# Moving softplus sums to TensorE and a share of the C products to GpSimd in a fused Mamba and SwiGLU kernel

## What is computed

```python
u = _silu(conv(xs));  delta, Bm, Cm = split(u @ x_proj_w.T, [64, 80])
delta = softplus(delta @ dt_proj_w.T + dt_proj_b)
deltaA = exp(einsum('bld,dn->bldn', delta, A))
deltaB_u = (delta * u)[..., None] * Bm[:, :, None, :]
state = dA * state + dBu                  # over the 512 tokens
y = einsum('bdn,bn->bd', state, c)
y = (y + u * D) * _silu(res);  x = layernorm(x + y @ out_proj_w.T + x)
x = layernorm(x + (silu(x @ wg.T) * (x @ wu.T)) @ wd.T)
```

## Time and profile before

| | |
|---|---|
| median of 3 runs | 580.98 us (580.44 to 583.85) |
| the profiled execution | 581.86 us, span 580.1 us |
| mean granted TensorE clock | 0.898 of full speed |
| busy, of 580.1 us | VectorE 521.0, TensorE 476.2, GpSimd 417.0, ScalarE 367.2 |
| one scan of a group, VectorE | 1.21 us, 256 times |
| one product of a quad, GpSimd | 4.54 us, 63 times |
| one decay, ScalarE | 0.69 us (three in a row 1.91) |
| table load, SiLU of 128x512, Copy of 128x512, ScalarE | 1.28, 0.68, 0.60 us |
| C spread and B spread, TensorE, one record | 0.50 us, 0.42 from start to start |
| x1 part of the job down, 8 records | 1.05 us |
| filler, TensorE | 348 records, 102.5 us |

### The profile page before, as it was taken

How to read it: one execution, slowest core, us unless ns; L and a number is a source line. 1 busy time by engine, 2 the same in 40 slices (tenths; PEclk the granted TensorE clock), 3 DMA queues, 4 the chain that set the end, 5 groups by cost and what they waited for, 6 DMA issues and landing times.

```text
span 580.1 us, 6345 instructions
## 1 busy us (share of the span) xinstructions
PE 476.2 (82%) x1887; PEld 239.6 (41%) x1887; DVE 521.0 (90%) x562; ACT 367.2 (63%) x581; POOL 417.0 (72%) x214
## 2 busy tenths in 40 slices
PE   8988774989979996989978996989888996587574
PEld 6332431535542553534442553444443452243243
DVE  5869789998999899998999899999999899999924
ACT  3577865489458866589458866589458855544220
POOL 8758597857695796968695796868695796876010
PEclk9889976989979898989979897989979997769879
DMA  8063333600642032600551042501451042500000
GB/s 222 3 146 62 83 72 74 145 1 5 141 108 56 1 82 67 160 1 15 131 120 46 0 97 62 149 0 24 121 131 31 0 101 70 138 1 0 1 18 18
DMA packets 27368, 39.22 MB, mean 68 GB/s; under 512 B 3816, under 2 KB 10056, under 8 KB 27344
## 3 DMA queue, kind: packets, MB, share of 16 engines
q1 hardware_dynamic: 25424, 38.51, 27.9%
q10 hardware_dynamic: 1920, 0.42, 0.4%
HBM read 3.27 MB, written 2.10 MB: 9 GB/s over the span
## 4 chain that ended last, share of the span: by engine, by line
PE 27%; issue 23%; DVE 21%; POOL 18%; ACT 6%; DMA 2%; SPq 1%; POOLq 0%; DVEq 0%; ACTq 0%
DVE state L1038 14%; POOL prod L864 10%; PE dense_ps L464 6%; PE dense_ps L482 5%; PE y_ps L456 4%; DVE weighted L1046 3%; POOL z_wm L868 2%; ACT decay_ps L620 2%; POOL z_wm L870 2%; PE c_ps L442 1%; PE dense_ps L484 1%; PE dense_ps L506 1%; POOL z_wm L881 1%; PE dense_ps L502 1%; SPq L358 1%
## 5 line engine op out<-in xcount | busy, mean ns | idle before, releaser
L864 POOL TENSOR_TENSOR prod<-du_rep,b_rep 128x2048 f32<-128x2048 f32 x63 | 285.6, 4540 | 52.0 <-ACT b_rep L657 32.8
L1038 DVE TENSOR_TENSOR_SCAN state<-decay_ps,prod 128x512 f32<-128x512 f32 x256 | 299.1, 1207 | 19.5 <-ACT decay_ps L620 13.4
L620 ACT ACTIVATE decay_ps<-delta_rep,a_neg 128x512 f32<-128x512 f32 x252 | 170.6, 688 | 107.3 <-DVE state L1038 107.1
L1046 DVE TENSOR_TENSOR weighted<-state,c_ps 128x2048 f32<-128x2048 f32 x64 | 146.4, 2288 | 4.2 <-PE c_ps L442 2.3
L464 PE MATMUL dense_ps<-x_all,ident 128*128 128x256 f32 x348 | 102.5, 430 | 18.9 <-ACT bc L653 9.4
L464 PEld LDWEIGHTS dense_ps<-x_all,ident 128*128 128x128 f32 x348 | 67.1, 207 | 65.9 <-issue 21.2
L456 PE MATMUL y_ps<-weighted,gather 128*32 128x512 f32 x512 | 77.7, 683 | 17.0 <-DVE weighted L1046 17.0
L482 PE MATMUL dense_ps<-h_t,tap_t 128*128 128x512 f32 x128 | 58.5, 599 | 0.9 <-ACT h_t L668 0.9
L442 PE MATMUL c_ps<-bc,pick 64*128 64x512 f32 x64 | 34.7, 542 | 19.7 <-DVE weighted L1046 19.7
L442 PEld LDWEIGHTS c_ps<-bc,pick 64*128 64x128 f32 x64 | 12.8, 200 | 69.6 <-issue 38.5
L889 POOL TENSOR_TENSOR ve<-mv,epsm 128x4 f32<-128x4 f32 x14 | 2.8, 202 | 53.1 <-DVE mv L1057 53.1
(11 more groups left out here) (148 smaller groups left out, 628.6 us busy)
## 6 DMA issues: line engine op xcount, KB each, us to landing
du_rep<-z_wm SPq DMA_DIRECT2D x64, 256.0 KB, 4.7
delta_rep<-z_ln SPq DMA_DIRECT2D x64, 256.0 KB, 4.5
out_dram<-y_out SPq DMA_DIRECT2D x8, 256.0 KB, 2.2
state<-L_attn_in_proj_w_in ACTq DMA_DIRECT2D x1, 256.0 KB, 3.9
x_all<-L_attn_x_in SPq DMA_DIRECT2D x1, 256.0 KB, 4.3
weighted<-L_ffn_w_gate_in SPq DMA_DIRECT2D x1, 192.0 KB, 9.8
weighted<-L_ffn_w_up_in SPq DMA_DIRECT2D x1, 192.0 KB, 3.5
weighted<-L_ffn_w_down_in SPq DMA_DIRECT2D x1, 192.0 KB, 4.5
```

The lines of the kernel that those rows point to most:

```text
L620: A(decay_ps[n % DECAYS][:, :], decay_ps[n % DECAYS][:, :] if spread_first else delta_rep[:, h, c, :], ACT.Exp, scale=a_neg[:, col:col + 1 ...
L864: TT(prod[quad % 2][:, :, :], du_rep[:, h, :, :], b, ALU.mult).then_inc(prod_ready, 1)
L1038: dve.tensor_tensor_scan(state[n // BLOCKS % 2][:, n % BLOCKS, :], decay_ps[n % DECAYS][:, :], prod[n // BLOCKS % 2][:, n % BLOCKS, :], 0. ...
L1046: TT(weighted[quad % 2][:, :, :], state[quad % 2][:, :, :], c_ps[:, :].unsqueeze(1).broadcast_to([P, BLOCKS, T]), ALU.mult).then_inc(weigh ...
```

## The change

The same computation with another division of labour:

- Delta is summed by TensorE: two new jobs d0 and d1 add the four parts in PSUM by four products with the identity, and ScalarE copies the result out. `zwm` now gives 1 - w instead of w - 1. GpSimd's `error` and `soften` stay for the head alone.
- C is multiplied onto the state in place; `weighted` is gone. So a quad's first scan waits until the quad two before has been summed, where the multiply waited for that so far.
- In quads 0, 1, 4 and 5 GpSimd multiplies the first of the four blocks (`weigh_first`), from an SBUF copy of C that ScalarE makes at quads 0 and 1 (`hold_c`); VectorE multiplies the other three.
- PLAN, BANK, ACT_AT, DVE_AT, POOL_AT and the head's fillers are new. The 23 fillers of a steady batch become 5.

```diff
-        weighted = pair("weighted", [P, BLOCKS, T])
+        c_rep = sb("c_rep", [P, CHUNKS, T])
-        cut = room(weighted[0][:, :, :])
+        cut = room(state[1][:, :, :])
-        PLAN = [["Fh", "h", "S", "C", "proj", "xs0"],
...
+        PLAN = [["h", "C", "S", "proj"],
+                ["xs0", "C", "S", "Fxs1"],
+                ["xs1", "res0", "C", "res1", "S"],
+                ["xd", "Fz0", "Fz0", "C", "z0", "Fz1", "S", "z1", "Fx1", "x1"],
+                ["S", "gate0", "C", "d0"],
+                ["C", "S", "gate1", "up0", "d1", "gate2"],
+                ["S", "b0", "C", "up1", "up2", "down", "b1", "b2", "b3"],
+                ["S", "C"]]
+        BANK = {"h": 2, "xs0": 1, "proj": 2, "xs1": 0, "res0": 2, "res1": 1, "xd": 0, "z0": 2, "z1": 0, "x1": 0,
+                "gate0": 2, "up0": 0, "gate1": 2, "up1": 1, "gate2": 2, "up2": 0, "b0": 0, "b1": 1, "down": 2,
+                "b2": 2, "b3": 1, "d0": 0, "d1": 1}
+        ACT_AT = {"hx": 0, "y": 8, "h": 0, "r1": 5, "silu": 10, "xd": 11, "x1n": 14, "z": (14, 15), "x1": 18,
+                  "ze": 18, "zw": 19, "zwm": 19, "ln": 20, "gate": (19, 22, 25), "b": (26, 29, 29, 30), "down": 27,
+                  "d": (21, 25), "c": 2}
+        DVE_AT = {"combine": (17, 2), "stats1": 9, "gate": (19, 23, 25), "up": (24, 26, 26), "stats2": 29}
+        POOL_AT = {1: ["C0"], 2: ["C1"], 3: ["norm1"], 4: ["low"], 5: ["C4", "scale0"], 6: ["C5"], 7: [],
+                   8: ["scale1", "norm2"]}
+        STIR_HEAD = {"h": 12, "xs0": 1, "du0": 3}
+        SHARED = [0, 1, 4, 5]
+        HELD = sorted({quad % CHUNKS for quad in SHARED})
+        def shares(quad):
+            return sum(q < quad for q in SHARED)
             def spread_c(it, quad):
                 it.wait(pe, weighted_ready, QUADS, 0, quad)
+                if quad > 0 and quad - 1 in HELD:
+                    it.wait(pe, c_held, len(HELD), 0, HELD.index(quad - 1) + 1)
             def sum_states(it, quad, batch=0):
...
+                if quad in SHARED:
+                    it.wait(pe, share_ready, len(SHARED), batch, shares(quad + 1))
...
+                elif kind == "d":
+                    it.wait(pe, z_step, 4, 1, 3)
+                    mm(ps[:, :], ident[:, :], z_e[:, n, :], start=True, stop=False)
+                    it.wait(pe, wm_ready, 1, 1, 1)
+                    mm(ps[:, :], ident[:, :], z_wm[:, n, :], start=False, stop=False)
+                    it.wait_taken(pe, f"z{n}")
+                    mm(ps[:, :], ident[:, :], z_pos[:, n, :], start=False, stop=False)
+                    it.wait(pe, ln_ready, 1, 1, 1)
+                    last = mm(ps[:, :], ident[:, :], z_ln[:, n, :], start=False, stop=True)
+            def take_delta(it, h):
+                name = f"d{h}"
+                it.wait_full(act, name)
+                it.take(A(delta[:, h, :], it.ps(name)[:, :], ACT.Copy), name)
+            def hold_c(it, q):
+                it.wait(act, c_ready, QUADS, 0, q + 1)
+                it.wait(act, share_ready, len(SHARED), -1, shares(q + CHUNKS + 1))
+                A(c_rep[:, q, :], c_ps[:, :], ACT.Copy).then_inc(c_held, 1)
-                        A(z_wm[:, :, :], z_w[:, :, :], ACT.Copy, bias=-1.0).then_inc(wm_ready, 1)
+                        A(z_wm[:, :, :], z_w[:, :, :], ACT.Copy, scale=-1.0, bias=1.0).then_inc(wm_ready, 1)
+            def weigh_first(it, quad):
+                it.wait(pool, scanned, GROUPS, 0, BLOCKS * quad + 1)
+                it.wait(pool, c_held, len(HELD), 0, HELD.index(quad % CHUNKS) + 1)
+                TT(state[quad % 2][:, 0, :], state[quad % 2][:, 0, :], c_rep[:, quad % CHUNKS, :], ALU.mult
+                   ).then_inc(share_ready, 1)
             def scan(it, n):
                 if n % BLOCKS == 0:
-                    it.wait(dve, weighted_ready, QUADS, 0, n // BLOCKS - 1)
+                    it.wait(dve, summed, QUADS, 0, n // BLOCKS - 1)
+                    if it.k0 == 0 and n == BLOCKS:
+                        dve.wait_ge(ffn_float, 3)
             def weigh(it, quad, batch=0):
-                it.wait(dve, summed, QUADS, batch, quad - 1)
                 it.wait(dve, c_ready, QUADS, batch, quad + 1)
-                TT(weighted[quad % 2][:, :, :], state[quad % 2][:, :, :],
-                   c_ps[:, :].unsqueeze(1).broadcast_to([P, BLOCKS, T]), ALU.mult).then_inc(weighted_ready, 1)
+                if quad in HELD:
+                    it.wait(dve, c_held, len(HELD), batch, HELD.index(quad) + 1)
+                mine = slice(1 if quad in SHARED else 0, BLOCKS)
+                TT(state[quad % 2][:, mine, :], state[quad % 2][:, mine, :],
+                   c_ps[:, :].unsqueeze(1).broadcast_to([P, BLOCKS - mine.start, T]), ALU.mult
+                   ).then_inc(weighted_ready, 1)
```

More of the change, by code:

```diff
@@ L220, in mamba_swiglu_postln @@
         weighted_ready = sem("weighted_ready")
+        c_held = sem("c_held")
+        share_ready = sem("share_ready")
         summed = sem("summed")
@@ L239, in mamba_swiglu_postln @@
         y_free = [sem(f"y_free{i}") for i in range(2)]
-        PLAN = [["Fh", "h", "S", "C", "proj", "xs0"],
[7 rows of a table removed]
-        BANK = {"h": 1, "xs0": 1, "proj": 2, "xs1": 0, "res0": 2, "res1": 1, "xd": 2, "z0": 0, "z1": 2, "x1": 0,
-                "gate0": 1, "up0": 2, "gate1": 0, "up1": 1, "gate2": 2, "up2": 0, "b0": 0, "b1": 1, "down": 2,
-                "b2": 0, "b3": 2}
-        ACT_AT = {"hx": 0, "y": 9, "h": 0, "r1": 5, "silu": 10, "xd": 13, "x1n": 14, "z": (15, 16), "x1": 18,
-                  "ze": 17, "zw": 18, "zwm": 19, "ln": 21, "gate": (19, 20, 21), "b": (24, 28, 29, 30), "down": 28}
@@ L255, in mamba_swiglu_postln @@
-        DVE_AT = {"combine": (21, 2), "stats1": 9, "gate": (19, 21, 22), "up": (20, 23, 25), "stats2": 29}
-        POOL_AT = {1: [], 2: [], 3: ["norm1"], 4: ["low"], 5: ["error0", "error1", "soften0"],
-                   6: ["soften1", "scale0"], 7: [], 8: ["scale1", "norm2"]}
-        STIR_HEAD = {"h": 11, "xs0": 2, "du0": 2}
+        PLAN = [["h", "C", "S", "proj"],
[6 more added lines that the diff above has]
+                ["S", "C"]]
@@ L320, in wait_free, with wait_delta @@
                     eng.wait_ge(taken[self.bank(name)], value)
+            def wait_delta(self, eng, h):
+                if self.k0 < 0:
+                    eng.wait_ge(delta_ready, h + 1)
+                else:
+                    self.wait_taken(eng, f"d{h}")
             def ps(self, name):
@@ L455, in sum_states @@
                 for c in range(BLOCKS):
-                    last = mm(y_ps[DB * c:DB * c + DB, :], gather[:, :], weighted[quad % 2][:, c, :],
+                    last = mm(y_ps[DB * c:DB * c + DB, :], gather[:, :], state[quad % 2][:, c, :],
                               start=False, stop=(q == CHUNKS - 1), tile_position=(0, DB * c))
@@ L683, in dense @@
                         if step == at["z"][h]:
-                            if h == 0:
+                            if h == 0 and it.k0 == 0:
                                 it.wait(act, delta_ready, HALVES, 0, HALVES)
@@ L706, in dense @@
                     A(z_ln[:, :, :], z_e[:, :, :], ACT.Ln, bias=1.0).then_inc(ln_ready, 1)
+                if it.ins:
+                    for h in range(HALVES):
+                        if step == at["d"][h]:
+                            take_delta(it, h)
+                if it.scan and step % BLOCKS == at["c"] and step // BLOCKS in HELD:
+                    hold_c(it, step // BLOCKS)
                 if it.k0 == 0:
@@ L877, in scale_u @@
             def scale_u(it, h):
-                it.wait(pool, delta_ready, HALVES, 1, h + 1)
+                it.wait_delta(pool, h)
                 if h == HALVES - 1:
@@ L929, in iteration @@
                             scale_shift(it, mv2, mv2_ready, ve2, nm2, ve2_ready, rs2, rs2_ready, nmr2, shift2_ready)
+                        if name[0] == "C" and it.scan and int(name[1]) in SHARED:
+                            weigh_first(it, int(name[1]))
                         if name == "low" and it.ins:
@@ L932, in iteration @@
                         for h in range(HALVES):
-                            if name == f"error{h}" and it.ins:
-                                error(it, h)
-                            if name == f"soften{h}" and it.ins:
-                                soften(it, h)
                             if name == f"scale{h}" and it.ins:
```

2 lines of the change are left out of this document (1 added, 1 removed), and 7 rows, old and new, of the table PLAN.

## The result

| | before | after |
|---|---|---|
| median, runs alternating on one chip | 581.44 us (578.69 to 584.54) | 586.64 us (584.77 to 587.45) |
| profiled span | 580.1 us | 584.9 us |
| mean granted TensorE clock | 0.898 | 0.843 |

What follows compares the result with a forecast made beforehand. It took VectorE as full, with TensorE, ScalarE and GpSimd queues arriving with under 0.2 us to spare. 1.0 - 6 x 0.2 - 1.6 + 1.2 = -0.6 from 581.86 gave 581.3, median 580 us; range 566 to 592, the forecast's own 575 to 587.

Steps and rivals of the forecast that it cites:

- 1, scan 4: Scan 4 still waits for GpSimd's product 1, T+7.45 (T: start of scan 0); quad 0's saving is lost.
- 2, scan 8: Four scans (4.59 us) and a narrower multiply (2.21 less 0.53) put scan 8 at T+13.7.
- 3, scan 12: Quad 2 as before, 7.93 us without its wait: scan 12 at T+21.65.
- 4, xd copy: ScalarE copies xd at T+21.7, before at T+23.54; scan 13 therefore waits 0.5 to 0.9 us.
- 5, logarithm ends: ScalarE takes 16.95 us from xd copy to logarithm, formerly 18.66; it ends at T+38.65, 3.5 us earlier.
- 6, stall of 1.7 before scan 22: Scan 22's decay, behind logarithm and table load, is ready at T+40.6; VectorE, there at T+38.9, stalls 1.7 us.
- 7, scan 24: GpSimd's product 6 follows delta copy 0 and scale0, ending T+46.95; scan 24 at T+47.05, before T+48.79.
- 8, up2 taken; down's end: TensorE's queue behind the logarithm takes 17.1 us: up2 done on VectorE at T+52.85, down ends T+55.9.
- 9, product 0; period: ScalarE's copies and decays reach T+59.9, then product 0 ends at T+64.5; period 64.6 us, 0.2 less.
- Rival 1: VectorE stays the bound, waits stay 3.1 us per batch: 566 us in full, 573 by half; chance 0.28.
- rival 2: TensorE falls to half clock after idling, delaying delta products or the queue behind: period 66.3, 591 us; chance 0.3.
- Rival 3: Narrow in-place multiplies don't pay, costing 0.5 us more a quad: 583 to 587 us; chance 0.07.

Runs made afterwards that it cites:

- e6: Changed kernel, but in batch 0, quad 0, VectorE multiplies all four blocks and GpSimd none: 585.53 us, ratio 1.0099 to the kernel before.
- e3: Changed kernel with six more filler jobs on TensorE between z1 and the x1 filler: 586.31 us, ratio 1.0096 to the kernel before.
- e9: Kernel before with only the in-place C multiply shared with GpSimd; softplus, TensorE order and fillers as before: 584.82 us, ratio 1.0088.
- e12: e9 without the ten TensorE fillers between gate product 2 and up product 2: 582.85 us, ratio 1.0036 to the kernel before.
- e2: Changed kernel with the share undone, VectorE multiplying all four blocks of every quad with C: 588.57 us, ratio 1.0137 to the kernel before.
- e5: Changed kernel with gates and ups going round three PSUM banks in the closing batch alone: 583.31 us, ratio 1.0059 to the kernel before.
- e7: Changed kernel without three of the four products of delta job 1 (less than the whole computation): 597.53 us, ratio 1.031 to the kernel before.

## Why the prediction was wrong

The sign was wrong: 1 us faster was forecast, 5 slower came. The steps that failed are terms of the sum that were mis-sized: batch 0 (+1.0, measured +2.29), the six periods (-1.2, measured +1.18), the last scanned batch (-1.6, measured -0.63) and the closing one (+1.2, measured +1.96). Behind them stands a reading that was wrong as well, of what bounds the kernel.

**The steps of the period.** Measured against T = 167.57, in the order of the prediction:

| step | predicted | measured |
|---|---|---|
| 1, scan 4 | T+7.45 | T+7.41 |
| 2, scan 8 | T+13.7 | T+13.68 |
| 3, scan 12 | T+21.65 | T+21.55 |
| 4, xd copy | T+21.7 | T+21.77 |
| 5, logarithm ends | T+38.65 | T+38.95 |
| 6, stall of 1.7 before scan 22 | yes | no: VectorE had lost 1.82 at the combine |
| 7, scan 24 | T+47.05 | T+47.44 |
| 8, up2 taken; down's end | T+52.85; T+55.9 | T+53.3; T+56.3 |
| 9, product 0; period | T+59.9; 64.6 | T+60.42; 64.99 |

The mechanism was right: GpSimd behind the copy of delta, TensorE's queue behind the logarithm. The products queued behind it took 17.3 us (206.57 to 223.83) where 17.1 were worked out. The sum is late by 0.3 us at the logarithm (step 5), 0.4 at scan 24 and 0.5 at product 0. Over the five periods from batch 2 on the mean is 64.88 us, 64.83 before: +0.05 where -0.2 was forecast, 1.3 us of the error. The first period, 65.68, is 0.9 longer than before and makes 1.1 more; it was taken to be like the others, and what lengthens it is open (e6 only shows that it grows when batch 0 ends sooner). The text had said that "0.5 us in one is 3 us", and took the middle. Step 6's stall was right in kind: e3 shows it, at 1.73 us, where the clock is repaired.

**The analysis of the bound failed.** "VectorE is full, but three queues arrive with less than 0.2 us to spare" takes the queues for guests. e9 shows them to be the bound: with 1.9 us less on VectorE the period is 64.80 as before. Rival 1, at 0.28, deserved next to nothing, and the chance of slower more. The 3.1 us of waits in the earlier trace rows were the mark: an engine that waits 3.1 us in each turn is not the longest path by itself, the path is one that runs through those waits. In the rows that I had, product 0 waited 4.99 us for a b_rep copy; I noted it as nearly late, and it is on one of the paths that close. TensorE ran at half clock from 319 to 322; I used that for rival 2 alone, and by e12's short batches it was worth, with the stretch behind the beat, 2.1 us of every period of e9. In steady batches, then, the change could only gain by its order and by the clock. Its order brought 3.3 us at the logarithm and gave them back in d0, d1 and the sums queued behind it, as steps 7 and 8 said.

**The ends** make 3.0 of the 5.4 us of error. Batch 0 was sized at +1.0 and measured +2.29. The block of quad 0 costs its 1.23 us as worked out, but the u x delta of half 1 comes 1.98 us later than in the earlier trace rows, at 52.47: scan 3 is 0.73 us later, and GpSimd's first addition waits for VectorE's work behind it. Its decay stands on ScalarE behind h_t, which waits 2.69 us for TensorE where it waited 1.56; why TensorE comes later there is open, but it goes with the share: in e9 scan 3 is 0.51 us later, in e2, without the share, 0.41 us earlier (40.04), and there nothing of the 2.29 is left. In the changed kernel nothing comes back; scan 16 starts 1.91 us later (70.28):

```profile
42.80 1.28 POOL L914 TENSOR_TENSOR z_wm<-z_e,z_wm 128x512 f32<-128x512 f32 x1 [1.62 <-DVE z_wm L1075]
...
45.38 1.27 POOL L932 TENSOR_TENSOR state<-state,c_rep 128x512 f32<-128x512 f32 x1
...
52.47 1.27 POOL L927 TENSOR_TENSOR z_wm<-z_ln,u 128x512 f32<-128x512 f32 x1
```

The last scanned batch gave -0.63 where -1.6 was due; e9 gives exactly 1.6 with TensorE's old order, so the missing 1.0 us is the new order's (waits of 0.38 us for a C spread and 0.36 for a tanh, which e9 does not have; the other 0.2 is not located). The closing batch was predicted by the right cause, one bank for three gates, at +1.2; it took +1.96, within the 0.5 to 2 given: besides the wait of 1.41 us the stretch at half clock got longer. e5 takes 2.6 back.

**Rival 2, the clock.** Half clock did come back from T+29 to T+35, where I had put TensorE's idle time and one of the two signs for this rival, and the condition (a slow stretch past T+37.5) was not met: the delta products ran at 1.00. e3 shows that this stretch cost nothing. The Trainium skill's page "TensorE: Matmul & The Clock Gate", section "HAM oscillation — how this bites in real kernels", was cited for 591. The traces agree in part. In the changed kernel a wait of 3.09 us is followed by a stretch at 0.51, which had slack around it. In e7 a wait of 1.78 us is followed by such a stretch, which cost 3 us, and one of 1.71 us in the next batch is not; in e12 the stretch comes in every second batch and costs 5 us against its neighbours. **Rival 3** fell: a narrow multiply in place costs 1.754 us, the 0.53 less that were worked out.
